# A graph network on one core: dense block counts per pass (58/56 instead of 57 throughout), an early start of block 0 in two passes, and node work in another order

## The reference

```python
h = relu(layernorm(x)); x = x + L0(h)     # two rounds: h_self and segment_sum((x@W0+b0)[src], dst), then W2, then / std
h = relu(layernorm(x)); x = x + L1(h)     # segment_sum(x[src] @ W + b, dst) / degree
h = relu(layernorm(x)); x = x + L2(h)     # three rounds: norm-weighted segment_sum(h[src], dst) @ W + b
h = relu(layernorm(x)); x = x + L3(h)     # an MLP on every edge, times edge_attr, segment_sum, an MLP on every node
```

## Time and profile before

| | |
|---|---|
| runs | 7783.07 us median of 3 (7775.79 to 7784.93) |
| the profiled execution | 7780.93 us, span 7779.1 us, mean granted clock 0.961 |
| PE busy | 6960.1 us (89%) |
| POOL busy | 5398.6 us (69%) |
| DVE busy, ACT busy | 3609.6 us (46%), 1612.6 us (21%) |
| pass 0, first to last amat store | 177.0 to 1380.7 us |
| first dense matmul of passes 1, 2, 3, 4, 5 | 1406.9, 2310.9, 3182.5, 4031.7, 4880.9 us |

### The profile page before, as it was taken

The page is one execution under the profiler, slowest core; times in us unless marked ns, Lnnn a source line. Parts: engine busy times, 40 slices in busy tenths (PEclk is TensorE's granted clock), DMA queues, the critical chain, the costliest instruction groups (busy, mean ns, idle before and its releaser), DMA issues.

```text
span 7779.1 us, 139548 instructions
## 1 busy us (share of the span) xinstructions
PE 6960.1 (89%) x53778; PEld 5623.6 (72%) x53778; DVE 3609.6 (46%) x7497; ACT 1612.6 (21%) x3217; POOL 5398.6 (69%) x5559
## 2 busy tenths in 40 slices
PE   2999999899989999999999999999987777777787
PEld 1677777787777777777877777777766666666676
DVE  7888988334442333333322333333344444444444
ACT  4777777111110000000000000010111111111111
POOL 0466666677657777677767777677747777777776
PEclk9999999999999999999999999999988999899898
DMA  7334333666565666655665556666545555555554
GB/s 152 116 129 133 132 123 132 187 191 188 182 200 185 198 196 192 206 183 181 191 207 179 185 186 188 205 193 187 185 154 148 146 146 148 143 151 145 149 144 131
DMA packets 568381, 1306.54 MB, mean 168 GB/s; under 512 B 223636, under 2 KB 326359, under 8 KB 560471
## 3 DMA queue, kind: packets, MB, share of 16 engines
q1 hardware_dynamic: 295076, 810.67, 31.5%
q0 software_dynamic: 177744, 371.65, 18.5%
q10 hardware_dynamic: 94948, 115.60, 4.3%
HBM read 1097.44 MB, written 207.42 MB: 168 GB/s over the span
## 4 chain that ended last, share of the span: by engine, by line
PE 53%; POOL 19%; issue 8%; DMA 3%; DVE 3%; ACT 0%; ACTq 0%; SPq 0%; DVEq 0%; POOLq 0%
PE PS L2451 41%; POOL GF L826 19%; PE PS L2431 5%; DMA work<-amat 2%; PE PS L2598 1%; PE PS L2297 1%; PE PS L2306 1%; PE PS L2516 1%; PE PS L2438 1%; PE PS L2316 0%; PE PS L2293 0%; PE PS L2457 0%; PE PS L2292 0%; DVE work L1839 0%; PE PS L2295 0%
## 5 line engine op out<-in xcount | busy, mean ns | idle before, releaser
L2451 PE MATMUL PS<-PARTS,work 128*128 128x288 bf16 x27930 | 3617.2, 288 | 66.9 <-issue 44.9
L2451 PEld LDWEIGHTS PS<-PARTS,work 128*128 128x128 fp8e4 x27930 | 2747.0, 99 | 760.2 <-issue 83.0
L837 POOL DMA_INDIRECT GF<-newparts,SRC x1640 | 1563.5, 953 | 687.9 <-issue 493.9
L837 POOL DMA_INDIRECT work<-newparts,SRC x1655 | 1576.7, 953 | 540.6 <-issue 498.3
L826 POOL DMA_INDIRECT GF<-table,SRC x1563 | 1475.0, 944 | 532.5 <-issue 475.7
L821 POOL DMA_INDIRECT GF<-newparts,SRC x659 | 749.9, 1138 | 505.0 <-PE PS L2538 202.1
L2598 PE MATMUL PS<-PARTS,work 128*128 128x289 bf16 x5586 | 999.0, 289 | 0.0
L1190 ACT ACTIVATE work<-PS 128x396 fp8e4<-128x396 f32 x1824 | 865.5, 500 | 290.3 <-PE PS L2516 246.2
L1913 DVE TENSOR_REDUCE FREE<-PS 128x96 f32<-128x288 f32 x415 | 189.7, 457 | 1431.1 <-PE PS L2431 1419.1
L2378 PE MATMUL PS<-work,QW 128*96 128x512 bf16 x1173 | 395.9, 455 | 427.8 <-DMA GF<-table,SRC 388.6
L1839 DVE TENSOR_TENSOR work<-PS,REL 128x1024 bf16<-128x1024 f32 (+1 forms) x611 | 741.3, 1214 | 0.3 <-issue 0.3
(11 more groups left out here) (293 smaller groups left out, 5892.0 us busy)
## 6 DMA issues: line engine op xcount, KB each, us to landing
work<-amat SPq DMA_DIRECT2D x285, 896.0 KB
work<-amat SPq DMA_DIRECT2D x285, 672.0 KB
work<-in_dst_dram SPq DMA_DIRECT2D x195, 512.0 KB
amat<-work SPq DMA_DIRECT2D x57, 1568.0 KB, 5.8
work<-in_edge_attr_dram SPq DMA_DIRECT2D x195, 384.0 KB
GF<-newparts,SRC POOLq DMA_INDIRECT x2299
PARTS<-newparts SPq DMA_DIRECT2D x35, 1008.0 KB, 10.0
work<-newparts,SRC POOLq DMA_INDIRECT x1655
```

Of the source, the lines that this page charges most:

```text
L837: pool.indirect_dma_start(GP[place_of(g)][:, i, :], None, part_rows[a % 2], bass.IndirectOffsetOnAxis(ap=SRC[:, tile:tile + 1], axis=0)).t ...
L2451: last = pe.matmul(PS[:, dense_bank(d), 0:PQ], AB[m][:, jj * WIN:(jj + 1) * WIN].bitcast(FP8), PARTS[:, j * PQ:j * PQ + PQ], start=(j == 0 ...
```

## The change

The number of dense blocks becomes a number of the pass: 58 in passes 0, 2, 3 and 4 (`DG` 115, 81 groups gathered, SKIP 7), 56 in passes 1 and 5 (111, 85 groups, SKIP 3). The table is built for 58 blocks; for the groups 111 to 114, which the short passes gather although the table covers their first edges in part, a masked copy of the destinations (`RELM`) leaves out what block 55 has already added. A slot then holds 4.6 pieces in passes 1 and 5 and 5.0 in passes 2 to 4.

In passes 1 and 5 the `PARTS` pieces 3 and 6 are loaded in two portions each, and PE begins block 0 with the 85 tiles that do not need the last units (`early_tiles`), goes on with pieces 0 to 2 of block 1, and then adds the 13 tiles left (`late_tiles`). Block 1's tables come in three DMAs instead of two: pieces 0 to 2, piece 3, pieces 4 to 6.

Node work: ACT does the units of a slot in the order of q, so that a new unit's `stage` stands ahead of the old one's `second_part`; the product of l0b comes after the slot's fifth piece (or its last); and in l2c DVE runs its chain after the first two pieces' events instead of at the slot's start, and PE turns the result in the next slot.

```diff
-DB = 57
-DG = 113
+DB = 58
+DG = 115
 HEAD, SKIP = DB - SPLIT, DG - 108
 GG = GROUPS - DG
+
+PASS_BLOCKS = (58, 56, 58, 58, 58, 56)
+PASS_HEADS = [b - SPLIT for b in PASS_BLOCKS]
+PASS_DG = [DG - 2 * (DB - b) for b in PASS_BLOCKS]
+PASS_SKIP = [g - 108 for g in PASS_DG]
+PASS_GROUPS = [GROUPS - g for g in PASS_DG]
...
+EARLY = {3: (42, 50, 56), 6: (84, 91, 98)}
+EARLY_PASSES = (1, 5)
...
-PIECES_FIRST, PIECES_TENTHS = 10, 48
-
-
-def pieces_before(t):
-
-    if t <= SKIP:
+PIECES_FIRST = 10
+
+
+def pieces_before(a, t):
+
+    slots = TURNS_SLOTS - 1 - PASS_SKIP[a]
+    if t <= PASS_SKIP[a]:
         return 0
-    return min(DB * AC, PIECES_FIRST + (t - 1 - SKIP) * PIECES_TENTHS // 10)
+    tenths = -(-10 * (PASS_BLOCKS[a] * AC - PIECES_FIRST) // slots)
+    return min(PASS_BLOCKS[a] * AC, PIECES_FIRST + (t - 1 - PASS_SKIP[a]) * tenths // 10)
...
-PRODUCT_AFTER = {"l0b": 1, "l1": 1, "l2a": 1, "l2b": 1, "l2c": 1}
+PRODUCT_AFTER = {"l0b": 4, "l1": 1, "l2a": 1, "l2b": 1, "l2c": 1}
...
+            def late_parts(a):
+                if a < 3:
+                    sp.wait_ge(S["uns"], done(S, "uns", a))
+                sp.wait_ge(S["par"], 16 * done(S, "par", a))
+                if a not in EARLY_PASSES:
+                    load_parts(a, EARLY)
+                    return
+                for m in EARLY:
+                    sp.wait_ge(p_ld[m], parts_landed(a, m, False))
+                    load_part_tiles(a, EARLY[m][1], EARLY[m][2], p_ld[m])
+                load_pieces(a, 1, 3, 1, d_ld[0])
+                load_pieces(a, 1, 4, 3)
 
...
-                        if m not in (3, 6):
+                        sp.wait_ge(d_mm, BLOCKS_BEFORE[a] * AC + m + 1)
+                        if m not in EARLY:
                             load_parts(a, (m,))
+                        elif a in EARLY_PASSES:
+                            load_part_tiles(a, EARLY[m][0], EARLY[m][1], p_ld[m])
                         for first, n in LOADS:
                             if m == first + n - 1:
-                                load_pieces(0, a * DB, first, n)
-                    if a < 3:
-                        sp.wait_ge(S["uns"], done(S, "uns", a))
-                    sp.wait_ge(S["par"], 16 * done(S, "par", a))
-                    load_parts(a, (3, 6))
+                                load_pieces(a, 0, first, n)
+                    if a in EARLY_PASSES:
+                        load_pieces(a, 1, 0, 3)
+                    late_parts(a)
                 with sp.Else():
...
+                    units = units_in(a, t)
+                    if PHASES[a + 1] == "l2c":
+                        for half, u, q in units:
+                            if q == 3:
+                                rows_and_first(S, a + 1, half, u)
+                    for half, u, q in sorted(units, key=lambda unit: unit[2]):
...
-                one_hot(tiles_of[k], REL[:, bass.ds(g * TPG + first * TPG, TPG)], places).then_inc(done, 1)
+                rel = REL[:, bass.ds(g * TPG + first * TPG, TPG)]
+                if first and g + first < DG:
+                    rel = RELM[:, (g + first - LEAST_DG) * TPG:(g + first - LEAST_DG + 1) * TPG]
+                one_hot(tiles_of[k], rel, places).then_inc(done, 1)
...
+                def first_halves(units):
+                    for half, u, q in units:
+                        if q == 1:
+                            step(S, a + 1, q, False, half, u)
+
                 def slot(t):
-                    pieces = range(pieces_before(t), pieces_before(t + 1))
-                    blocks = max(0, (pieces_before(t) - TURN_AT - 1) // AC)
-                    if t > SKIP:
-                        add_window(t - 1 - SKIP, (t - 1) % 2, blocks)
-                    for half, u, q in units_in(t):
-                        step(S, a + 1, q, False, half, u)
-                    for piece in pieces:
+                    pieces = range(pieces_before(a, t), pieces_before(a, t + 1))
+                    blocks = max(0, (pieces_before(a, t) - TURN_AT - 1) // AC)
+                    if t > skip:
+                        add_window(t - 1 - skip, (t - 1) % 2, blocks)
+                    units = units_in(a, t)
+                    for half, u, q in units:
+                        if q != 1:
+                            step(S, a + 1, q, False, half, u)
+                    if not pieces:
+                        first_halves(units)
+                    for k, piece in enumerate(pieces):
                         d, m = divmod(piece, AC)
                         if m == TURN_AT and d:
-                            add_block(d - 1, max(0, t - SKIP))
+                            add_block(d - 1, max(0, t - skip))
                         if m == AC - 1:
                             sum_parts(d)
-                    if t >= SKIP:
+                        if k == min(PRODUCT_AFTER[PHASES[a + 1]], len(pieces) - 1):
+                            first_halves(units)
...
-                if after and (q == 2 and name in ("l1", "l2a", "l2b") or q == 1 and name == "l2c"):
+                if after and q == 2 and name in ("l1", "l2a", "l2b"):
...
+                def tile_sums(d, first, end):
+
+                    for j in range(first, end):
+                        m, jj = divmod(j, piece_tiles)
+                        last = pe.matmul(PS[:, dense_bank(a, d), 0:PQ], AB[m][:, jj * WIN:(jj + 1) * WIN].bitcast(FP8),
+                                         PARTS[:, j * PQ:j * PQ + PQ], start=(j == 0), stop=(j == NT - 1))
+                    return last
...
+                def early_tiles():
+
+                    pe.wait_ge(d_add, b0 + 1)
+                    for m in range(AC):
+                        if m in LOADED:
+                            pe.wait_ge(d_ld[m], tables_landed(a, 0, m))
+                        pe.wait_ge(p_ld[m], parts_landed(a, m, False))
+                        pe.nop(nofuse=True)
+                        last = tile_sums(0, m * piece_tiles, EARLY[m][1] if m in EARLY else (m + 1) * piece_tiles)
+                        if m < 3:
+                            last.then_inc(d_mm, 1)
+
+                def late_tiles():
+
+                    pe.wait_ge(p_ld[3], parts_landed(a, 3))
+                    tile_sums(0, EARLY[3][1], EARLY[3][2]).then_inc(d_mm, 1)
+                    pe.wait_ge(p_ld[6], parts_landed(a, 6))
+                    tile_sums(0, EARLY[6][1], EARLY[6][2]).then_inc(d_mm, 3 + PIECES_FIRST - AC)
...
+                        if p == 0 and a in EARLY_PASSES:
+                            early_tiles()
+                        if d == 0 and a in EARLY_PASSES:
+                            continue
                         if p == AC:
                             pe.wait_ge(S["read"], done(S, "read", a))
                             name = "hts" if a < 3 else "ev"
                             pe.wait_ge(S[name], done(S, name, a))
                         piece(d, m)
-                        if p == first and t > SKIP:
+                        if p == PIECES_FIRST - 1 and a in EARLY_PASSES:
+                            late_tiles()
...
+                        if q == 2 and PHASES[a + 1] == "l2c":
+                            turned(a + 1, half, u)
```

198 lines of the change are left out of this document (115 added, 83 removed).

## The result

The changed kernel takes 7706.3 us (median of 6 runs, 7702.1 to 7710.8) against 7781.4 (6 runs, 7775.8 to 7792.0): ratio 0.9903, 95% interval 0.989 to 0.9916, so 75 us or 1.0% less. I had forecast 44 us less. The profiled execution has a span of 7700.2 us, 78.9 less than that of before.

What follows compares the result with a forecast made beforehand. The prediction took POOL to bound passes 2 to 4 and PE passes 0, 1 and 5. Its terms, +18 - 23 - 6 - 33 = -44 us, gave a forecast of 7738 us, range 7715 to 7766.

Steps and rivals of the forecast that it cites:

- What bounds the kernel: POOL holds passes 2 to 4, by only about 12 us each; PE holds passes 0, 1 and 5.
- Passes 2 to 4, -6.2: Passes 2 to 4: PE gains its waits for gathered rows, pays 9.9 us each; together -6.2 us, bounds +29.7 and -12.
- POOL waiting 5 to 12 us per pass in 2 to 4: A sign to look for in passes 2 to 4: POOL waits 5 to 12 us per pass, PE's waits there gone.
- Pass 1, -23: Pass 1: POOL's limit of -25.3 us, less 2 for two engines so close; -23 us, bounds -25.3 and -13.
- Pass 5, -33: Pass 5: block exchange -9.9 and PE's waits -24.2, near POOL's limit of -36; -33 us, bounds -36 and -10.
- the first rival: Node work: waits only move to the next instruction; DVE's chain may hold up `window` in l2c; 7770 us, chance 0.12.
- Pass 0, +18: Pass 0: +17 us for the extra block less two groups, +1 for small DVE operations in setup and masks.
- the reordered node work brings nothing: Node work on ACT, DVE and PE: the waits are only moved to the next instruction; 7770 us, chance 0.12.
- Middle passes pay the block in full: Passes 2 to 4: the 36 us before gathered sums come back before other lines; 7773 us, chance 0.08.
- tables no longer keep up: Passes 2 to 4: PE waits for table loads, 0.5 us in each of 174 blocks, +87 us; 7825, chance 0.04.
- Better than forecast: POOL's limits are reached in both short passes and the long ones lose further waits; 7725 us, chance 0.2.

Runs made afterwards that it cites:

- mid57: The changed kernel with 57 blocks and 83 gathered groups in passes 2 to 4 instead of 58 and 81; 7744.3 us, ratio 0.9947 to the kernel before.
- light57: mid57 with the last of every group's 8 gathers left out in passes 2 to 4, PE's work unchanged; 7693.9 us, ratio 0.9876 to the kernel before.
- light58: The changed kernel, 58 blocks kept, without the last of every group's 8 gathers in passes 2 to 4; 7716.4 us, ratio 0.9905 to the kernel before.
- short57_no_reorder: The changed kernel with 57 blocks in passes 1 and 5 and the node work in its old order; 7770.3 us, ratio 0.9977 to the kernel before.
- dve_old: The changed kernel with only DVE's part of the node work's new order undone; 7732.7 us, ratio 0.9925 to the kernel before.
- act_old: The changed kernel with only ACT's part of the node work's new order undone; 7715.2 us, ratio 0.9904 to the kernel before.
- no_reorder: The changed kernel with the node work back in its old order on ACT, DVE and PE; 7741.3 us, ratio 0.9941 to the kernel before.

## Why the prediction came out as it did

- **What bounds the kernel**: right. POOL held the middle passes, PE the short ones. What I took from the earlier trace rows as the size of POOL's hold, "only about 12 us each", was too small. The listed waits for gathered rows are 11.4, 9.4 and 15.1 us, 36 in all; by mid57 and light57 the hold is 57. In mid57, with passes as long, the same waits come to 42: PE's waits before products and for tables came to 18.9 us in the middle passes of the kernel before and to 12.9 in mid57, and since POOL set the length of these passes, the 6 us only moved to the line of the gathered sums. The other 15 us are no waits at all but busy time, which a table of waits can't show.
- **Passes 2 to 4, -6.2**: this term failed, by 31 us of the 36 by which the passes (79.8 us together) miss the sum of 44. Its step was "PE gains at most its waits for gathered rows and pays 9.9". PE gained 57 where I had 36, and paid 18.7 in length where I had 29.7. The gain was short by 5 us of waits that stood at other lines and by some 16 us of busy time, the matmuls that ran at the lower clock or were cut off by a stop. The price itself was sound as work (9.5 of busy time), but 10 us of it went into PE's remaining idle time. My bounds allowed 12 us for smaller waits and nothing for busy time.
- **"POOL waiting 5 to 12 us per pass in 2 to 4"**: wrong, though PE did become the limit. POOL has four buffers and PE ended 6 to 10 us behind its last gather, so nothing ever filled up. A pass can be PE's without one recorded wait on POOL; only light58, where POOL waits 100 to 104 us a pass, made it visible.
- **Pass 1, -23**: -29.5. The last gathered sum is 853.8 us behind the first gather instead of 880.1, so 26.2 us, POOL's limit of 25.3 and a little; the 2 us that I took off for two level engines weren't lost. The other 3 us lie behind the last group. The wait moved to block 2 as forecast (2.8 us before its table), though SP issued that table at 1449.95 and it landed at 1463.0, not at 1452; and the six waits for `stage` went. The start, which I had at 3.5 us, is worth 9 to 10 where PE is the limit (901.7 against 910.7 us, 875.5 against 885.9) and nothing where POOL is. But short57_no_reorder says that the swap and the reorder each bring most of it alone, which my addition of -9.9 and -14.2 did not say.
- **Pass 5, -33**: -29.7. POOL never waits and the last sum is 31.5 us earlier after the first gather; POOL's limit was 36, and POOL itself took 2.5 us longer for its 675 tiles than at the 1.259 us of the earlier trace rows (851.1 us from first to last start). The reasons hold in part: the sum's wait for DVE, 7.9 us in the earlier trace rows, was the one that mattered, more than its size (dve_old: 21 us); the waits for `stage` were not (act_old: 2 us, less than single executions differ). As the first rival said, DVE's chain now holds up `window` at the slot's end: 7.2 us, half hidden by POOL.
- **Pass 0, +18**: +16.7, with the wrong parts: the block and the setup about 13, the early tiles 3.7.
- **The rivals**: "the reordered node work brings nothing" is refuted by no_reorder (+31 us). "Middle passes pay the block in full" and "tables no longer keep up" are refuted by pass 3, where the waits for tables fell from 6.1 us to 1.4. "Better than forecast" is what came, by its second half, "the long ones lose further waits", and went past its 7725 and past the 7715 at which my range ended.
- **The clock** went as the earlier trace rows let expect: the time at the lower level fell from 61 to 29 us in pass 1 and from 45 to 29 in pass 5. It fell in the middle passes too, where I had left it out, from 65 to 50 us. The Trainium skill's page "TensorE: Matmul & The Clock Gate", section "What's actually happening", says that the array's clock falls when the array has been idle and that activity brings it back. The traces agree: with 41 us of pauses gone between mid57 and light57 the time at the lower level falls from 54 to 42 us. By the estimate above that is 6 us, only a part of the 16.5.

## What to carry to other kernels

Where one engine feeds another, the waits at the line that takes the fed data were less than what the feeder cost: here 42 us of 57 in the same kernel (36 in the one before), because PE's stops, and the lower clock that came with them, also lengthened its busy time. A kernel that lightens the feeder alone measures the whole. Price a swap from busy times, but let it first fill the idle time that is left on the engine that pays. Two edits that both free the same engine don't add up in the pass where either is enough, and an edit that brings nothing at one balance can carry the next step (the reorder: 0 us in pass 2 with 57 blocks, 11 us with 58, which is ACT's part).

## What the chip showed that was not expected

Some of POOL's gathers are longer than 0.94 us. Two pieces of the timeline in pass 3 of the changed kernel, POOL's and DVE's at the same moment:

```profile
3432.94 0.94 POOL L893 DMA_INDIRECT work<-newparts,SRC  x1 [0.30 <-issue]
3434.18 1.25 POOL L893 DMA_INDIRECT work<-newparts,SRC  x1 [0.30 <-issue]
3435.74 0.94 POOL L893 DMA_INDIRECT work<-newparts,SRC  x1 [0.30 <-issue]
...
3433.28 0.65 DVE L1667 TENSOR_TENSOR work<-PS,DINV 128x480 f32<-128x480 f32 x1
3433.96 0.66 DVE L1672 TENSOR_TENSOR work<-work,W 128x480 f32<-128x480 f32 x1
3434.65 0.66 DVE L1707 SCALAR_TENSOR_TENSOR work<-work,DINV 128x480 f32<-128x480 f32 x1
```

The long gather ends at 3435.43, 0.81 us behind the end of DVE's line 1672 (3434.62), which was under way when it began. I compared all long gathers of passes 1 to 5 (over 0.98 us, 212 of 3279) with DVE's instructions: every one ends 0.81 to 0.83 us behind the end of a DVE instruction of the node work, always one of seven lines that take both inputs from SBUF (1672, 1707, 1724, 1732 and three more; one of these, 1624, in one of its two uses). Six gathers that begin within 0.04 us behind the start of such an instruction, with 0.59 us and more of it to go, keep their 0.94 us. Gathers that begin under an instruction with an input in PSUM (391 under the one-hot of line 1906, 193 under the reductions of lines 1970 and 1984, 40 under line 1667) are not long (the two more under line 1906 that are had line 1724, with both inputs in SBUF, begin at the same time). The Trainium skill's page "SBUF — State Buffer", section "Who interferes with whom", states that a DVE instruction with two inputs in SBUF contends with a GpSimd instruction that reads SBUF. The trace agrees, if a gather's reading of its indices (`SRC`) is such a read; that it is this read was not tried.

What it costs: in pass 4 POOL has 47 long gathers and takes 812.9 us from the first to the last start; without the reorder 21 and 804.4 us. It is ACT's part of the order that brings them: act_old has 10 in this pass, dve_old 45. By which way was not followed up. A gather of the middle passes costs 1.266 to 1.267 us instead of the 1.259 that I had taken from the earlier trace rows. It did not change the time there, since PE sets these passes. Pass 5 is POOL's, and there 45 of 675 gathers are long and the last starts 851.1 us behind the first, in pass 1 29 and 847.2.
